# Moving the zero points, the identity rows and the triangular mask of a state-space block to other places

## What is computed

```python
x = x + cross_attention(layernorm(x), ctx, mask)          # 8 groups of 4 heads
x = x + mamba2(layernorm(x))
x = x + layernorm(x) @ (scale * (digits - zero)).T + bias

def mamba2(h):                                            # H = 128 heads, G = 8 groups, L = 128
    gate, hBC, dt = split(h @ in_proj.T)
    hs, B, C = split(silu(conv4(hBC)))                    # causal, 4 taps per channel
    dt = softplus(dt + dt_bias);  A_dt = -exp(A_log) * dt
    Lmat = exp(segsum(A_dt))                              # 0 above the diagonal
    M = (C @ B.T) * Lmat                                  # per head, scores of B and C shared by group
    y = M @ (hs * dt) + D * hs
    y = group_rms_norm(y * silu(gate)) * norm_weight
    return y @ out_proj.T
```

## Time and profile before

| what | us |
|---|---|
| three executions, median | 710.45 |
| their lowest and highest | 709.9, 710.72 |
| the profiled execution: its span, from the first to the last instruction | 707.5 |
| PE busy in that span | 696.7 |
| DVE, ACT, POOL busy | 547.0, 393.6, 297.4 |

### The profile page before, as it was taken

The page is one execution under the profiler, slowest core; times in us unless marked ns, Lnnn a source line. Parts: engine busy times, 40 slices in busy tenths (PEclk is TensorE's granted clock), DMA queues, the critical chain, the costliest instruction groups (busy, mean ns, idle before and its releaser), DMA issues. The chain is left out here.

```text
span 707.5 us, 12227 instructions
## 1 busy us (share of the span) xinstructions
PE 696.7 (98%) x4081; PEld 591.2 (84%) x4081; DVE 547.0 (77%) x1175; ACT 393.6 (56%) x602; POOL 297.4 (42%) x150
## 2 busy tenths in 40 slices
PE   8999999999999999999999999999999999999997
PEld 7888888888888888888888888879989898989976
DVE  5988578658748857866875884767999999999984
ACT  4564454535546446345553654653867676767752
POOL 3354223404504503331350440200288887888762
PEclk9999999999999999999999999999999999999999
DMA  9702022021001102202102100871677888787710
GB/s 324 269 21 76 1 74 74 0 74 59 15 19 63 66 0 74 74 0 74 59 15 74 59 0 0 315 311 61 236 273 300 314 312 329 300 333 300 279 57 16
DMA packets 20293, 93.77 MB, mean 133 GB/s; under 512 B 2608, under 2 KB 3760, under 8 KB 11440
## 3 DMA queue, kind: packets, MB, share of 16 engines
q1 hardware_dynamic: 20272, 93.50, 35.6%
HBM read 93.17 MB, written 0.33 MB: 132 GB/s over the span
## 5 line engine op out<-in xcount | busy, mean ns | idle before, releaser
L1468 POOL TENSOR_TENSOR wqo_lo<-wqo_raw,wqo_hi 128x2048 fp32r<-128x2048 f32 x15 | 69.6, 4643 | 192.2 <-ACT wqo_hi L754 163.4
L1132 DVE TENSOR_TENSOR pt_lo<-bank,pt_hi 128x512 fp32r<-128x512 f32 x128 | 87.7, 690 | 51.4 <-ACT pt_hi L828 50.8
L828 ACT ACTIVATE pt_hi<-bank 128x512 fp32r<-128x512 f32 x128 | 75.6, 598 | 57.0 <-PE bank L520 57.0
L1455 POOL TENSOR_TENSOR k_lo<-rope_a,k_hi 128x512 fp32r<-128x512 f32 x32 | 42.7, 1336 | 104.3 <-ACT k_hi L772 104.3
L1501 POOL TENSOR_TENSOR w_out_lo<-w_out_sb,w_out_hi 128x2048 fp32r<-128x2048 f32 x16 | 73.4, 4589 | 21.6 <-ACT w_out_hi L941 21.6
L1093 DVE CUSTOM_DVE_ANT_0 probs<-bank,mask_sb 128x512 f32<-128x512 f32 x128 | 82.0, 686 | 0.1
L520 PEld LDWEIGHTS bank<-ident_r,probs_r 128*128 128x128 f32 x512 | 55.7, 140 | 19.5 <-DVE pt_lo L1132 5.8
L1506 POOL TENSOR_TENSOR w_gate_lo<-w_gate_sb,w_gate_hi 128x2048 fp32r<-128x2048 f32 x14 | 64.7, 4619 | 16.7 <-ACT w_gate_hi L933 16.7
L818 ACT ACTIVATE probs<-probs,neg_max 128x2048 f32<-128x2048 f32 x31 | 61.9, 2003 | 0.8 <-DVE neg_max L1083 0.8
L612 PE MATMUL bank<-xnT,w_hs_sb 128*128 128x128 f32 x512 | 60.6, 277 | 0.0
L520 PE MATMUL bank<-ident_r,probs_r 128*128 128x128 f32 x512 | 57.8, 237 | 1.5 <-DVE pt_lo L1132 1.5
(11 more groups left out here) (197 smaller groups left out, 1722.7 us busy)
## 6 DMA issues: line engine op xcount, KB each, us to landing
w_hs_sb<-in_w_hs SPq DMA_DIRECT2D x16, 1024.0 KB, 4.9
w_out_sb<-in_w_out SPq DMA_DIRECT2D x16, 1024.0 KB, 6.7
w_gate_sb<-in_w_gate SPq DMA_DIRECT2D x16, 1024.0 KB, 4.9
wqo_raw<-in_wq SPq DMA_DIRECT2D x8, 1024.0 KB, 4.7
wqo_raw<-in_wo SPq DMA_DIRECT2D x8, 1024.0 KB, 4.8
decay<-decay_rows SPq DMA_DIRECT2D x16, 512.0 KB, 6.9
ctx_raw<-in_ctx_t SPq DMA_DIRECT2D x3, 1024.0 KB, 10.8
wk_raw<-in_wk SPq DMA_DIRECT2D x8, 256.0 KB, 2.6
```

The lines of the kernel that those rows point to most:

```text
L828: act.activation(pt_hi[t % 3], ring_b[(t + 1) % 2][:, :], ACT.Copy).then_inc(s["pt_hi_ready"], 1)
L1132: dve.tensor_tensor(pt_lo[t % 3], ring_b[(t + 1) % 2][:, :], pt_hi[t % 3].bitcast(F32), ALU.subtract)\
L1468: pool.tensor_tensor(wqo_lo[:, :, :], wqo_raw[:, :, :], wqo_hi[:, :, :].bitcast(F32), ALU.subtract)\
```

## The change

- `upper` is gone with its instruction on POOL; PE's first wait asks for one constant fewer. `make_gm` is gone: the scores are not masked. Instead the first column of the step decays is set to zero (POOL, one element per partition; ACT's Exp writes the other 127), so that the scan begins each head from zero. SP's store of the step decays waits for that memset too.
- `subtract_zeros` runs on POOL, four instructions in place on the integer digits, behind the second norm and ahead of `first_gate_lo`. `scale_weights` in the last chunk then reads the integer digits.
- The copy of the identity into `same_step_bank` is an ACT instruction behind the Exp of `A_log`.
- On DVE the first scan stands ahead of `conv_step(0, 0)`, and `ygT_low(0, 0)` moves from the end of chunk 0 to behind `x_dt` and `x_skip` of chunk 1.

```diff
@@ SP
+            sp.wait_ge(s["first_step_zero"], 1)
             sp.wait_ge(s["step_decay_ready"], 1)
@@ PE
-            pe.wait_ge(s["consts_ready"], 4)
+            pe.wait_ge(s["consts_ready"], 3)
@@ ACT
             act.activation(alog_bc[:, :], alog_bc[:, :], ACT.Exp).then_inc(s["neg_a"], 1)
+            act.activation(same_step_bank[:, :].rearrange("p (h l) -> p h l", h=4),
+                           ident[:, :].unsqueeze(1).broadcast_to([P, 4, P]), ACT.Copy).then_inc(s["same_step_ready"], 1)
...
-                    act.activation(step_decay[:, :], last_step_bank, ACT.Exp).then_inc(s["step_decay_ready"], 1)
+                    act.activation(step_decay[:, 1:], last_step_bank[:, 1:], ACT.Exp).then_inc(s["step_decay_ready"], 1)
@@ DVE
-            def subtract_zeros(rows):
-                dve.wait_ge(s["digits_ready"], 2)
-                for o in rows:
-                    dve.tensor_tensor(weights[:, o, :].rearrange("p (g k) -> p g k", g=QG),
-                                      digits[:, o, :, :].rearrange("p (g k) two -> p g (k two)", g=QG),
-                                      zero_sb[:, o, :].unsqueeze(2).broadcast_to([P, QG, DM // QG]), ALU.subtract)\
-                        .then_inc(s["digits_off"], 1)
...
             digits_of_weights()
-            subtract_zeros(range(KC))
...
-            dve.tensor_copy(same_step_bank[:, :].rearrange("p (h l) -> p h l", h=4),
-                            ident[:, :].unsqueeze(1).broadcast_to([P, 4, P])).then_inc(s["same_step_ready"], 1)
...
-            def make_gm():
...
-                                             weights[:, o, :].rearrange("p (g k) -> p g k", g=QG),
+                                             digits[:, o, :, :].rearrange("p (g k) two -> p g (k two)", g=QG),
...
+                if second:
+                    ygT_low(0, 0)
...
-                if not next_to_last:
+                if not next_to_last and not first:
                     ygT_low(n, i, last_chunk)
...
-            conv_step(0, 0)
-            make_gm()
             dve.wait_ge(s["same_step_ready"], 1)
             scan_decay(0, 0)
-            dve.wait_ge(s["gm_ready"], 2)
+            conv_step(0, 0)
+            dve.wait_ge(s["g_mm"], 1)
             decay_products(0, 0)
@@ POOL
-            pool.affine_select(out=upper[:, :], in_=ones[:, :], compare_op=ALU.is_ge, fill=0.0, base=0,
-                               pattern=[[1, P]], channel_multiplier=-1).then_inc(s["consts_ready"], 1)
...
+            def subtract_zeros():
+                pool.wait_ge(s["digits_ready"], 2)
+                for o in range(KC):
+                    q = digits[:, o, :, :].rearrange("p (g k) two -> p g (k two)", g=QG)
+                    pool.tensor_tensor(q, q, zero_sb[:, o, :].unsqueeze(2).broadcast_to([P, QG, DM // QG]), ALU.subtract)\
+                        .then_inc(s["digits_off"], 1)
+
+            pool.memset(step_decay[:, 0:1], 0.0).then_inc(s["first_step_zero"], 1)
+            subtract_zeros()
             pool.wait_ge(s["gate_hi_ready"], 1)
```

More of the change, by code:

```diff
@@ L90, in build @@
         ones = sb("ones", [P, P])
-        upper = sb("upper", [P, P])
         ones_r = sb("ones_r", [P, P], F32R)
@@ L261, in build @@
             bcast_mm bcast_ready attn_out_ready oproj_ready res_added small_in dequant_in dt_in gate_in0 gate_in1
-            hs_in0 hs_in1 bc_in0 bc_in1 wout_in0 wout_in1 dt_mm dt_step dt_act neg_a a_dt_ready bc_mm bc_tap bc_tap_added bc_conv
-            bc_act_ready aT_mm step_decay_ready decay_rows_stored decay_in0 decay_in1 same_step_ready scan_ready g_mm gm_ready
+            hs_in0 hs_in1 bc_in0 bc_in1 wout_in0 wout_in1 dt_mm dt_step dt_act neg_a first_step_zero a_dt_ready bc_mm bc_tap bc_tap_added bc_conv
+            bc_act_ready aT_mm step_decay_ready decay_rows_stored decay_in0 decay_in1 same_step_ready scan_ready g_mm
             digits_ready digits_off weights_ready wT_mm wT_ready hs_mm hs_tap hs_conv hs_act hsT_mm x_ready m_ready
@@ L1360, in chunk_dve @@
                 c = 2 * n + i
+                first = isinstance(n, int) and c == 0
+                second = isinstance(n, int) and c == 1
                 next_to_last = isinstance(n, int) and c == CH - 2
```

## The result

| | kernel before | changed kernel |
|---|---|---|
| median, first measurement, us | 710.17 (709.54 to 710.72, 4 runs) | 713.75 (713.22 to 714.39, 4 runs) |
| ratio | | 1.0049, 95% interval 1.0035 to 1.0063 |
| median, second measurement, us | 710.77 (24 runs) | 714.69 (712.04 to 715.95, 7 runs) |
| ratio | | 1.0046, 95% interval 1.0029 to 1.0062 |

What follows compares the result with a forecast made beforehand. PE bounds the kernel, busy 696.7 of 707.5 us, so only its few waits count. Convolution 3.5 us later, less 0.26 of vanished wait, gives 3.2; 710.45 + 3.2 = 713.65, say 713.6 us, range 711.2 to 715.2.

Steps and rivals of the forecast that it cites:

- the 3.2 us: Net delay forecast at PE: convolution 3.5 us later, less a 0.26 us wait of PE that disappears.
- Parts 1 and 2: Dropping `upper` at PE's start: worth 0; DVE's relief: `dt_x` starts 1.04 us earlier, taps end at most 0.26 earlier.
- Part 3: POOL's four subtractions, 1.30 us each, hold three DVE dt instructions, 3.0 us in all; `a_dt` ends at 494.85, not 491.86.
- Rival 3: POOL's four queued subtractions let no DVE instruction between them; `a_dt` at 495.2, time 714.0 us; chance 0.08.
- rival 4: POOL's subtractions are slow on integers, at twice 1.30 us each; `a_dt` at 499.9, time 718.6 us; chance 0.10.
- Part 4: On DVE, taps 13.40 us, scan 2.32, convolution 3.42; the convolution ends at 514.0, 3.5 us later than before.
- Part 5: Convolution's end through ACT and POOL to PE's gate product, 11.69 us; it starts at 525.7, PE arriving about 523.4.
- the shift stays to the end: Behind chunk 1 PE is dense, so the whole 3.2 us delay reaches the end of the kernel.
- Rival 1: POOL does not hold DVE's small instructions; the scan's order alone ends the convolution 1.8 us later, 712.0 us; chance 0.20.
- Rival 2: PE's early-chunk waits of 0.91 and 0.26 us go and no new one comes; 709.3 us; chance 0.08.
- the prediction's first reading of POOL: At chunk 1's gate product, POOL's low part ends at 522.13, PE starts at 522.18: POOL is already what PE meets.

Runs made afterwards that it cites:

- zeros_dve: Changed kernel with the zero points subtracted on DVE again, the scan still ahead of the convolution; 712.79 us, ratio 1.0040.
- late: Changed kernel with the first convolution ahead of the scan again and POOL's four subtractions behind `first_gate_lo`; 709.86 and 710.26 us, ratios 0.9989 and 0.9992.
- fill16: Changed kernel with sixteen identity transposes on PE ahead of chunk 1's gate product; 712.76 us, ratio 1.0037.
- b_scan_fill: Kernel before with the first scan ahead of the first convolution and sixteen identity transposes on PE ahead of chunk 1's gate product; 711.97 us, ratio 1.0015.
- b_scan: Kernel before with only the first scan put ahead of the first convolution; 712.89 us, ratio 1.0031.
- b_pool: Kernel before with only the four zero-point subtractions moved to GpSimd; 711.16 us, ratio 0.9998.
- conv_first: Changed kernel with the first convolution ahead of the first scan again; 710.41 us, ratio 1.0001.
- both_back: Changed kernel with the convolution ahead of the scan again and the zero points subtracted on DVE again; 710.07 us, ratio 0.9997.

## Why the prediction was right, and where it was not

The time, the sign and the chain of waits were right; the composition of the 3.2 us was not. The ratio makes the measured shift 3.5 us; the median before is lower by 0.28 with its fourth execution. Some starts in the changed kernel's profile look like hits on the forecast, 525.76 for the gate product (525.7) and 514.66 for `out_high` (514.6). That is only the late start of this execution: the forecast was made on the kernel before's profile, and aligned they are 524.41 and 513.31. By the prediction's own parts:

- **Parts 1 and 2 hold.** `upper` brought nothing that shows: PE's first deadline depends on a load, as said. DVE's relief did let `dt_x` start behind PE's projection alone (a wait of 1.46 us for L605). That the taps can't use all of a gain was shown by `zeros_dve`, to 0.01 us of the bound, and by `late`, where they wait for ACT as well.
- **Part 3, the holding right, its size too large.** The three instructions that follow `dt_x` are held, as forecast, by 0.23 + 0.86 + 0.86 = 1.95 us, and not by 0.8 + 1.1 + 1.1 = 3.0. The term that was mis-sized is GpSimd's instruction, taken at 1.30 from the earlier trace rows:

```profile
L1509 POOL TENSOR_TENSOR digits<-digits,zero_sb x4: 1055/1080/1503, 487.3 to 490.4; 128x512 int32<-128x512 int32 x4
```

  Its median is 1.08. One of the four took 1.50, and none did beside the convolution in `late` (4.13 us for the four, against 4.60), so here DVE holds GpSimd as well. The four end at aligned 490.58 instead of 491.15, and `a_dt` at 493.87 instead of 494.85. Of these 0.98 us, 0.57 is POOL's earlier end; the rest lies in the three rounded holds, whose sum lets the chain go on 0.5 us after POOL's end, where it went on 0.1 after. Rival 3, a queue that lets nothing between, and rival 4, slow integers, both fall with these rows. (Rival 3's bound is a little low: 491.15 less the 0.32 from `dt_x` to the next instruction, and 4.56 on top, is 495.4 and not 495.2.)
- **Part 4, right but for overlaps.** The scan starts 13.31 us after the taps and the convolution 2.24 after the scan, where the sum took the rows' full 13.40 and 2.32. With the 0.98 of part 3 that explains a convolution that ends at 512.74 instead of 514.0, but for 0.1 us.
- **Part 5, the chain right, one term missing.** From the convolution's end to the gate product 11.67 us passed, 11.69 were forecast. The forecast wait of about 2 us came out as 2.09, by luck: the gate product was 1.3 us too late in the forecast, but so, by 1.1, was PE's arrival, 523.4 against an aligned 522.32, a number for which the prediction shows no working. And "the shift stays to the end" left out what the matmuls do after 2.09 us of idling: in the profiled execution the clock fell to 0.50, 1.4 to 1.6 us. The mean clock is below 1.000 in 8 of 11 executions of the changed kernel, and `fill16` and `b_scan_fill` took it away. The 1.25 us too many of parts 3 and 4 and this missing term nearly cancel; that 713.6 met 713.75 is in part luck.
- **Rival 1, only the order counts,** was priced at 712.0 and held less likely. Its premise, that POOL does not hold DVE's small instructions, is wrong. Its size is the larger part: `b_scan` alone makes 2.2 us, with 1.87 at the gate product. What GpSimd adds is 0.54 there (2.23 - 1.69), where the forecast's sum had 514.0 - 512.3 = 1.7 at the convolution; by itself, in `b_pool`, it adds nothing that the time shows.
- **Rival 2, faster,** asked for a convolution that ends by 510.5. `conv_first` and `late` have one, and gain nothing, or 0.6 to 0.8 us at the edge of what the measurement tells: PE then meets POOL's `gate_low` after 0.78 us, as the prediction's first reading of POOL said.

Three things stay open. What the moved `ygT_low`, the removed mask and the copy on ACT are worth was not tried one by one. What decides whether the clock falls in an execution was not found. And whether `late` is really faster than the kernel before was not settled: two intervals, 0.9979 to 0.9998 and 0.9983 to 1.0001.

## What to carry to other kernels

When two steps of one engine are exchanged, ask which of them a chain through other engines starts from: here 2.3 us of scan ahead of a convolution crossed four engines and came out at PE's gate product as 1.7 to 1.9. Work that goes to an idle GpSimd can be free for GpSimd and not for VectorE; here it was better placed beside VectorE instructions that read PSUM than beside small ones that read SBUF alone. And a wait of TensorE that is made longer can cost more than its length; count in what the matmuls behind it would take at the lower clock.

## What the runs showed of the hardware

- TensorE's granted clock fell to 0.50 within the matmuls that followed a wait of 2.09 us, with another wait of 0.75 about 3 us before; 128x512 matmuls took 0.63 us instead of 0.39 for 2.6 us. With almost the same waits (0.74 and 2.11) it stayed at 1.00 in one profiled execution of `b_scan`, while eight of that kernel's ten executions show a mean clock below 1.000. `b_pool`, with waits of 1.28 and 0.29 us, shows 0.998 in 3 of 11 executions. With 1.94 us of transposes in the wait it stayed at 1.000 in 16 of 16, as it did in all 45 executions of `conv_first`, `both_back` and `late`, whose profiles show waits of 0.20 and about 0.78 us at that place.
- A GpSimd instruction on int32 with one broadcast input took 1.08 us for 128x512, less than the 1.30 of float32 with two full inputs.
- Beside four GpSimd instructions in a row, three VectorE instructions were held, by 0.23, 0.86 and 0.86 us, and one of the four took 1.50 us instead of 1.08.
